# A transformer-like block on one core: the order of VectorE's work in the steps of the first unit

## What is computed

```
x = x + 0.5 * (LN(x) @ W_q.T + bias)          # W_q dequantised from 6-bit fields
x = x + S4_0(LN(x))                           # causal convolution along the 512 columns + D * u
x = x + 0.5 * (LN(x) @ W_q.T + bias)
x = x + 0.5 * FFN(LN(x))
x = x + S4_1(LN(x))
x = x + 0.5 * FFN(LN(x))
FFN(z) = (silu(z @ W_gate.T) * (z @ W_up.T)) @ W_down.T      # 512 -> 1376 -> 512
```

## Time and profile before

| | us |
|---|---|
| median of 3 runs | 920.38 (916.86 to 920.75) |
| the profiled execution | 920.42 |
| its span, first to last instruction | 918.63 |
| TensorE busy with matmuls | 888.6 |
| VectorE busy | 619.8 |
| GpSimd busy | 365.2 |
| ScalarE busy | 313.5 |
| mean granted clock of TensorE | 0.989 of full |

### The profile page before, as it was taken

The page is one execution under the profiler, slowest core; times in us unless marked ns, Lnnn a source line. Parts: engine busy times, 40 slices in busy tenths (PEclk is TensorE's granted clock), DMA queues, the critical chain, the costliest instruction groups (busy, mean ns, idle before and its releaser), DMA issues.

```text
span 918.6 us, 11736 instructions
## 1 busy us (share of the span) xinstructions
PE 888.6 (97%) x4116; PEld 725.4 (79%) x4116; DVE 619.8 (67%) x1057; ACT 313.5 (34%) x517; POOL 365.2 (40%) x729
## 2 busy tenths in 40 slices
PE   7899999989999999999999999999999999999998
PEld 3777887777777787888888888888888778888876
DVE  7768778788888878555566786655656864544452
ACT  4423446633443444221223352222243512222211
POOL 4974467832323336232324453233243542222211
PEclk8989999999999999999999999999999999999999
DMA  8200000055676596556465665556455757566345
GB/s 329 91 1 1 1 1 2 1 226 180 238 272 223 216 330 181 153 180 177 133 185 145 189 181 172 184 136 193 150 164 164 227 157 225 191 206 206 126 147 174
DMA packets 41310, 148.27 MB, mean 161 GB/s; under 512 B 3490, under 2 KB 3746, under 8 KB 39844
## 3 DMA queue, kind: packets, MB, share of 16 engines
q0 software_dynamic: 29040, 100.93, 36.6%
q1 hardware_dynamic: 12212, 46.59, 13.7%
HBM read 117.36 MB, written 30.15 MB: 161 GB/s over the span
## 4 chain that ended last, share of the span: by engine, by line
PE 74%; DVE 13%; POOL 7%; issue 2%; DMA 2%; ACT 1%; SPq 0%; DVEq 0%; POOLq 0%; ACTq 0%
PE front L1436 14%; PE front L1438 13%; PE front L1437 13%; PE acc L1390 7%; PE acc L1392 7%; PE acc L1391 7%; PE front L468 3%; DVE weight_operands L600 2%; PE acc L1321 2%; PE acc L1322 2%; PE acc L1320 2%; DVE snapshots L1191 2%; POOL x_rows L748 2%; DVE hidden_lo L1231 2%; POOL rstd L450 1%
## 5 line engine op out<-in xcount | busy, mean ns | idle before, releaser
L1436 PE MATMUL front<-row_operands_hi,weight_operands 128*128 128x512 f32 x616 | 243.2, 395 | 8.2 <-DVE snapshots L1191 8.1
L1438 PE MATMUL front<-row_operands_hi,weight_operands 128*128 128x512 f32 x616 | 240.5, 390 | 0.0
L1437 PE MATMUL front<-row_operands_lo,weight_operands 128*128 128x512 f32 x616 | 240.4, 390 | 0.0
L1436 PEld LDWEIGHTS front<-row_operands_hi,weight_operands 128*128 128x128 f32 x616 | 116.0, 188 | 36.5 <-issue 10.1
L1390 PE MATMUL acc<-down_weights,hidden_hi 128*128 128x512 f32 x352 | 140.0, 398 | 3.9 <-DMA down_weights<-saved_down 2.0
L1191 DVE TENSOR_TENSOR snapshots<-front,snapshots 128x512 f32<-128x512 f32 x132 | 90.9, 689 | 78.3 <-PE front L1438 77.0
L1392 PE MATMUL acc<-down_weights,hidden_lo 128*128 128x512 f32 x352 | 137.4, 390 | 0.0
L1391 PE MATMUL acc<-down_weights,hidden_hi 128*128 128x512 f32 x352 | 137.2, 390 | 0.0
L1438 PEld LDWEIGHTS front<-row_operands_hi,weight_operands 128*128 128x128 f32 x616 | 116.0, 188 | 24.7
L1437 PEld LDWEIGHTS front<-row_operands_lo,weight_operands 128*128 128x128 f32 x616 | 116.1, 189 | 23.3
L820 POOL DMA_DIRECT2D weight_operands<-saved_weights x66 | 48.6, 736 | 185.5 <-PE front L1438 180.6
(11 more groups left out here) (177 smaller groups left out, 1349.3 us busy)
## 6 DMA issues: line engine op xcount, KB each, us to landing
weight_operands<-saved_weights POOLq DMA_DIRECT2D x33, 1280.0 KB, 6.4
down_weights<-saved_down POOLq DMA_DIRECT2D x77, 512.0 KB, 4.1
saved_weights<-weight_operands SPq DMA_DIRECT2D x11, 1792.0 KB, 8.2
weight_operands<-saved_weights POOLq DMA_DIRECT2D x33, 512.0 KB, 4.5
raw_weights<-wgu SPq DMA_DIRECT2D x11, 512.0 KB, 4.3
saved_down<-down_weights SPq DMA_DIRECT2D x11, 512.0 KB, 3.4
x_rows<-x_in SPq DMA_DIRECT2D x3, 1024.0 KB, 11.6
out<-x_rows SPq DMA_DIRECT2D x3, 1024.0 KB, 5.1
```

Of the source, the lines that this page charges most:

```text
L1436: T.matmul(o, wh, xh, start=(j == 0), stop=False)
L1437: T.matmul(o, wh, xl, start=False, stop=False)
L1438: last = T.matmul(o, wl, xh, start=False, stop=(j == 1))
```

## The change

In the first unit's steps the low part of the fourth weight sum is made behind the reads of M4 and M3 and ahead of `hidden_lo`, and the statistics behind `hidden_lo`. TensorE waits for two low parts ahead of M6 and for the third ahead of M3. The store of the second half of unit 2 is issued as four transfers of one tile each.

```diff
--- before.py
+++ after.py
@@ -593,9 +593,12 @@
             nc.vector.tensor_tensor(raw_block(k, S4), raw_block(k, A12), raw_block(k, S2), ALU.subtract
                                     ).then_inc(w_step, 1)
 
-        def weight_lows(dve, k):
+        RAW, SUMS, FOURTH = range(3)
+
+        def weight_lows(dve, k, parts):
             dve.wait_ge(w_step, 4 * k + 4)
-            for i, (first, last) in enumerate(((A22, A12 + 1), (S2, S3 + 1), (S4, S4 + 1))):
+            for i in parts:
+                first, last = ((A22, A12 + 1), (S2, S3 + 1), (S4, S4 + 1))[i]
                 dve.wait_ge(w_hi, 3 * k + i + 1)
                 nc.vector.tensor_tensor(flat(W, k, LO, first, last), flat(Wr, k, LO, first, last),
                                         flat(W, k, HI, first, last).bitcast(F32), ALU.subtract).then_inc(w_ready, 1)
@@ -683,13 +686,13 @@
                         load_raw(k + 2)
                     if k + 1 < FT:
                         save_weights(k + 1)
-                    if u == 3 and f == 2:
-                        store(2, 1, 0, BLK)
+                    if u == 3 and f in (2, 4, 6, 8):
+                        store(2, 1, f // 2 - 1, f // 2)
                 if u >= 2:
                     store(u, 0, 0, BLK)
             for r in range(BLK):
                 store(3, 1, r, r + 1)
-            sp.wait_ge(stored, 16 * (3 + BLK))
+            sp.wait_ge(stored, 16 * (2 + 2 * BLK))
 
 
         @block.gpsimd
@@ -1182,7 +1185,7 @@
                 if n == PRE - 5:
                     weight_sums_b(dve, 0)
                 if n == PRE - 3:
-                    weight_lows(dve, 0)
+                    weight_lows(dve, 0, (RAW, SUMS, FOURTH))
 
             def add(k, product, read, out, other):
 
@@ -1248,20 +1251,28 @@
                         weight_sums_b(dve, k + 1)
                     middle_sums_c(k)
                     if k + 1 < FT:
-                        weight_lows(dve, k + 1)
+                        weight_lows(dve, k + 1, (RAW, SUMS))
                     if f == 0 and u:
                         for r in range(BLK):
                             ffn_update(u - 1, 1, r)
                     if 2 <= f < 2 + EMBEDDED[u]:
                         update_step(dve, embedded_item(u, f - 2))
-                    for n in STATS_OF_STEP[u][f]:
-                        stats_step(dve, n)
-                        aggregate_step(dve, n)
+                    if u:
+                        for n in STATS_OF_STEP[u][f]:
+                            stats_step(dve, n)
+                            aggregate_step(dve, n)
                     if 1 <= f <= EMBEDDED[u]:
                         xt_lo_step(dve, embedded_item(u, f - 1))
                     first_hidden(k)
                     second_gate(k)
+
+                    if k + 1 < FT:
+                        weight_lows(dve, k + 1, (FOURTH,))
                     hidden_lo(q, g0)
+                    if u == 0:
+                        for n in STATS_OF_STEP[u][f]:
+                            stats_step(dve, n)
+                            aggregate_step(dve, n)
                 q1 = PASSES * u + FT
                 hidden_lo(q1, H1[:, 0, :])
                 for r in range(BLK):
@@ -1456,7 +1467,7 @@
                     if f == 0:
                         pe.wait_ge(sums_lo, 4 * BLK * (u + 1))
                     if k < FT:
-                        pe.wait_ge(w_ready, 3 * k + 3)
+                        pe.wait_ge(w_ready, 3 * k + 2)
                     pe.wait_ge(snap_done, k + 1)
                     product(k, M6, S2, T2)
                     pe.wait_ge(front_read, READS * k + C11)
@@ -1477,6 +1488,8 @@
                         pe.wait_ge(w_last_in[k % 2], 16 * ((k - FT) // 2 + 1))
                     pe.wait_ge(front_read, READS * k + T_SUM)
                     product(k, M4, A22, T4N)
+                    if k < FT:
+                        pe.wait_ge(w_ready, 3 * k + 3)
                     pe.wait_ge(front_read, READS * k + C22)
                     product(k, M3, S4, B22)
                     if f == FT - 1:
```

## The result

| | before | after |
|---|---|---|
| median (us) | 920.20 of 7 runs (916.86 to 921.81) | 914.45 of 7 runs (910.26 to 915.06) |
| the profiled execution | 920.42 | 915.06 |
| its span | 918.63 | 913.3 |
| mean granted clock of TensorE | 0.989 | 0.993 |

The ratio of the times is 0.9931, with a 95% interval from 0.9913 to 0.9948: faster by 0.7%, some 6 us.

A forecast was written before the change was run, and what follows sets the result against it. TensorE, 97% busy, sets the floor, losing time waiting for VectorE's late read of M4. Eight borders at 1.00, plus 0.22 and 0.33, give 8.55 us: 920.42 to 911.9, range 908.5 to 916.5.

The forecast's parts named there:

- Fourth part and statistics behind the read of M4: First unit's steps: VectorE reads M4 earlier, TensorE's idle time goes, 13.24 falls to 12.24 us; eight borders gain 1.00 each.
- The border from step 0: First unit: idle time shrinks from 2.18 to 1.85, gaining 0.33 us; slow clock assumed to stay, 0 to 1.6 kept for range.
- Collision: Rival, first unit's steps: hidden_lo loses 1.09 us to GpSimd's multiplication at the shared port, total 915.9; chance 0.09.
- Who waits for what moved: First unit's steps: waiters on the moved VectorE work, including SyncE's later saving of weights, lose nothing.
- a rival with a chance of 0.08 and a time of 914: First unit's end: step 10's later weight saving holds GpSimd's queue; down weights late once, up to 2 us; chance 0.08.
- the term of the late saving: First unit: SyncE's saving of weights leaves about 1.3 us after M1 instead of 0.33 before; counted as nothing.
- Raw weights: First unit's steps: weight sums start sooner after the load, 0.5 us to spare, no cost; slower rival 925, chance 0.03.
- The store: Fourth unit: four pieces leave some 0.6 us apart, no TensorE wait behind them; zero, 0.3 us either way.
- No effect: Rival, first unit's borders: some other wait holds M1 at its present place, 920; chance 0.05.

The follow-up runs named there:

- experiment 3: Changed kernel, but only the statistics go behind hidden_lo; all three low parts stay ahead of the read of M4: 913.40 us, ratio 0.9927.
- experiment 4: Changed kernel, but only the fourth low part goes behind the reads of M4 and M3; the statistics stay where they were: 918.50 us, ratio 0.9986.
- Experiment 5: Changed kernel, but behind the read of M3 the order is statistics, fourth low part, hidden_lo: 919.58 us, ratio 0.9993.
- experiment 1: Changed kernel, but in step 9 alone the fourth low part is again ahead of the read of M4, so the last saving leaves early: 912.26 us.
- experiment 2: Changed kernel, but in step 10 GpSimd issues pass 12's down weights ahead of step 12's first operands; the saving stays late: 913.32 us, ratio 0.9928.
- experiment 7: Changed kernel with the early last saving, plus first-half stores of units 2 and 3 cut into four paced pieces: 908.54 us, ratio 0.9875.

## Why the prediction was right or wrong

*Fourth part and statistics behind the read of M4: right.* 12.24 us a step was forecast and measured, with the new order to within 0.07 us: 0.33 us of idle time left for 0.35, hidden_lo 0.50 ahead of GpSimd for 0.49, M1 in its turn. Experiments 3 and 4 give the two parts by themselves, 12.44 and 12.91, as the sum had them (0.82 and 0.33 off 13.24). Borders: 7.90 for 8.00, and 0.21 for 0.22.

*The border from step 0: right in the idle time (1.81 for 1.85), open in the clock.* The 1.6 us that I kept for the range came, as 1.5, in the profile after: 1.88 less the 0.33. It was luck: the same kernel's clock fell or did not fall there from one profile to the next (last section), and without it the profiled execution, 915.06, would have taken about 916.6, just outside the range.

*Collision: rightly a rival, rightly not the forecast.* Experiment 5 shows that it is real and costs 5.7 of the 7.9 us that the steps gain. The Trainium skill (SBUF — State Buffer, section "SBUF: two separate sides") says that a GpSimd instruction that reads SBUF and a VectorE one with two SBUF inputs exclude each other and that the first to start goes through; the 0.68 against 1.78 us of hidden_lo agree. The bank reads were weaker evidence than I took them for the earlier trace rows: in the kernel before, a read of M2 lies beside that multiplication for 0.1 us only, and in experiment 5 it starts 0.6 us behind the multiplication's end.

*Who waits for what moved: the step that failed.* I wrote that behind the saving "stands only the next loading of down weights", and looked at SyncE's queue alone. What waits for the saving on GpSimd's queue I saw, but booked under a rival with a chance of 0.08 and a time of 914 instead of in the sum. The runs put it at 1.2 to 1.8 us in five profiles and 3.8 in one, where the wait was the longest and the clock fell on top. I had written against it that no matmul waits for a transfer there today; the right question was how much lead the down weights had. They were issued at 332.95 with a load ahead of them of 1.3 MB issued at 330.53, landed 5.4 us later and were needed 6.7 us later. A saving 2 us later takes that load into them, and they had 1.3 us in hand. So the step that failed is the term of the late saving, put at nothing in the sum. With 1.7 in it the sum would have been 6.85 us, 913.6; the changed kernel's two medians are 914.45 and 912.56.

*Raw weights: right.* In the kernel after, the times from issue to landing of the raw weights' line (least, median and most):

```profile
DMA to landing us min/median/max: 3.5/4.0/15.2
```

The median is 4.0 us (4.3 before), and the sums never waited.

*The store: right*, ratio 1.0001. *No effect:* did not come.

## What to carry to other kernels

When an engine has idle time a little behind the point at which another waits for it, move work from before the urgent read into that idle time: it is worth what the timeline of one border says (7.9 us for 8.0 here), until the floor is reached. Then follow what the moved work releases: not only who waits on it now, but every queue that stands in order behind that waiter, and how much lead the transfers there have. And where two engines exclude each other, as VectorE and GpSimd did in experiment 5, half a microsecond of order can cost most of it.

## What was not expected of the hardware

**The clock behind an idle time of about 2 us.** It fell in some profiles and not in others, and not by the length of the idle time. TensorE's first matmul of step 1 in experiment 1 (idle 1.80) and in experiment 3 (idle 2.15), and the stretches of 3.5 us that follow, with the matmuls in parentheses:

```profile
199.33 0.58 PE L1447 MATMUL front<-row_operands_hi,weight_operands 128*128 128x512 f32 x1 [1.80 <-DVE snapshots L1194]
```

```profile
202.05 0.47 PE L1444 MATMUL front<-row_operands_hi,weight_operands 128*128 128x512 f32 x1 [2.15 <-DVE snapshots L1194]
```

```profile
199.33:202.80 3.47, 3.47 (x9) 2.72 (x10) 2.11 (x4) 1.83 (x3) 1.32 (x1) 0.53 1.01 361
```

```profile
202.05:205.50 3.45, 3.45 (x15) 2.88 (x16) 2.20 (x4) 1.72 (x3) 1.29 (x1) 1.00 1.00 306
```

With 1.80 the clock stood at the 1.2 GHz level for nearly all of the stretch (mean 0.53, 9 matmuls), with 2.15 at 2.4 GHz (15). Over eleven profiles: idle 1.80 to 1.81, fallen in two of seven; 2.15 to 2.18, in two of four. What else decides is open. It is worth 1.5 us, and may be one part of the 4 to 6 us by which runs of one kernel differ here. So my bounds on that term, between a wait of 1.75 and one of 2.18, bounded nothing.

**Step 5.** In the changed kernel and in experiments 1, 2, 4, 5 and 7 the read of M2 in step 6 comes 0.35 us late (12.59 us behind the last, in the changed one), in the kernels with all low parts together it does not. TensorE's products are not late there; VectorE stands idle for 0.68 us and not 0.33. In the changed kernel it costs 0.17 us over two steps (12.59 and 12.06 against 12.24 each); its cause is open.
